# GpSimd waits for a landing after every third of its indirect transfers, in a two-layer kernel with experts

## What is computed

```python
x = x + 0.5 * L0_ffn(norm(x))      # block 0: 8 experts, F = 344, silu(g) * u, top 2
x = x +       L0_attn(norm(x))     # block 1: RWKV-like, a scan over the tokens
x = x + 0.5 * L0_ffn(norm(x))      # block 2: as block 0
x = x + 0.5 * L1_ffn(norm(x))      # block 3: 8 experts, H = 512, silu, top 2
x = x +       L1_attn(norm(x))     # block 4: retention, 16 heads of 8
x = x + 0.5 * L1_ffn(norm(x))      # block 5: as block 3
```

## Time and profile before

| what | us |
|---|---|
| median of three runs | 818.75 |
| lowest and highest | 818.47, 823.67 |
| the profiled execution | 820.56 |
| its span, first to last instruction | 818.7 |
| mean granted TensorE clock in it | 0.886 |
| DMA packets | 45119, 50.19 MB |
| of them in POOL's queue (software_dynamic) | 11776, 24.14 MB |

### The profile page before, as it was taken

How to read it: one execution, slowest core, us unless ns; L and a number is a source line. 1 busy time by engine, 2 the same in 40 slices (tenths; PEclk the granted TensorE clock), 3 DMA queues, 4 the chain that set the end, 5 groups by cost and what they waited for, 6 DMA issues and landing times.

```text
span 818.7 us, 12941 instructions
## 1 busy us (share of the span) xinstructions
PE 633.4 (77%) x4180; PEld 540.2 (66%) x4180; DVE 387.9 (47%) x1056; ACT 342.5 (42%) x667; POOL 387.3 (47%) x400
## 2 busy tenths in 40 slices
PE   2478977997489786887867875899967999966782
PEld 2377767787467785876766875766743558856772
DVE  6442115696549661514240304079688785410202
ACT  2334545654266343343445542632321324633451
POOL 1544755454544345536355354572212285456532
PEclk9998997999699898769889887999977999979887
DMA  9641122012301113112032013110030011212203
GB/s 339 198 145 34 36 71 56 27 33 62 81 27 29 23 56 91 36 49 45 28 97 65 28 36 84 38 37 8 20 87 8 21 37 33 59 39 85 61 27 113
DMA packets 45119, 50.19 MB, mean 61 GB/s; under 512 B 14456, under 2 KB 36344, under 8 KB 45056
## 3 DMA queue, kind: packets, MB, share of 16 engines
q0 software_dynamic: 11776, 24.14, 12.3%
q1 hardware_dynamic: 33280, 25.23, 9.7%
HBM read 32.04 MB, written 17.29 MB: 60 GB/s over the span
## 4 chain that ended last, share of the span: by engine, by line
PE 48%; another core or an unknown queue 10%; DVE 8%; issue 5%; ACT 4%; DMA 2%; POOL 1%; ACTq 1%; DVEq 0%; SPq 0%; POOLq 0%
PE bank L612 13%; PE bank L599 9%; PE bank L592 8%; PE pair L700 4%; PE pair L732 3%; PE bank L573 2%; PE pair L526 1%; DVE hT L1252 1%; PE pair L536 1%; ACT w_up L831 1%; DMA xs<-tokens_in,idx_in 1%; ACT hT L852 1%; PE pair L516 1%; PE bank L615 1%
## 5 line engine op out<-in xcount | busy, mean ns | idle before, releaser
L1086 POOL DMA_INDIRECT tokens_out<-ys,idx_out x184 | 189.5, 1030 | 241.4 <-ACT ys L899 194.2
L1076 POOL DMA_INDIRECT xs<-tokens_in,idx_in x184 | 188.1, 1022 | 167.3 <-PE bank L573 59.2
L612 PE MATMUL bank<-w,hT 128*128 x1288 | 191.8, 296 | 52.2 <-ACT hT L852 20.3
L612 PEld LDWEIGHTS bank<-w,hT 128*128 128x128 f32 x1288 | 175.3, 208 | 69.5 <-issue 68.6
L592 PE MATMUL bank<-xT_kept,w_up 128*128 128x128 f32 x1104 | 173.9, 307 | 47.1 <-ACT gate L849 13.2
L592 PEld LDWEIGHTS bank<-xT_kept,w_up 128*128 128x128 f32 x1104 | 157.9, 218 | 65.8 <-issue 34.7
L831 ACT ACTIVATE w_up<-w 128x728 f32 (+1 forms) x184 | 129.3, 718 | 47.1 <-DVE owner L1232 19.0
L1252 DVE TENSOR_TENSOR hT<-gate,bank 128x384 f32<-128x384 f32 x92 | 50.7, 552 | 177.0 <-PE bank L592 75.3
L599 PE MATMUL bank<-xT_kept,w_up 128*128 128x128 f32 x736 | 107.3, 296 | 17.7 <-ACT hT L852 8.1
L599 PEld LDWEIGHTS bank<-xT_kept,w_up 128*128 128x128 f32 x736 | 98.1, 207 | 26.4 <-issue 17.8
L852 ACT ACTIVATE hT<-bank 128x512 f32<-128x512 f32 x92 | 54.6, 595 | 109.9 <-PE bank L599 50.6
(11 more groups left out here) (169 smaller groups left out, 626.0 us busy)
## 6 DMA issues: line engine op xcount, KB each, us to landing
yg<-tokens_out SPq DMA_DIRECT2D x64, 128.0 KB
w<-in_w SPq DMA_DIRECT2D x8, 536.0 KB, 8.4
w<-in_w SPq DMA_DIRECT2D x8, 512.0 KB
xs<-tokens_in,idx_in POOLq DMA_INDIRECT x184
tokens_out<-ys,idx_out POOLq DMA_INDIRECT x184
tokens_in<-xn SPq DMA_DIRECT2D x8, 256.0 KB
tokens_in<-xn SPq DMA_DIRECT2D x8, 254.0 KB
out<-x SPq DMA_DIRECT2D x8, 128.0 KB
```

Source lines behind the costliest of these rows:

```text
L612: last = mm(y, hT[0:n_f, n % 2, c * P:(c + 1) * P], w_of(k, e, WD[k] + c * P, P, n_f), start=(c == 0), stop=(k == 0 and c == CH[k] - 1))
L1076: pool.indirect_dma_start(xs[:, j % RING, :], None, xn_dram[KIND[f]][b], tile_rows(idx_in, b, j))\
L1086: pool.indirect_dma_start(ys_dram[b], tile_rows(idx_out, b, j), ys[:, j % RING, :], None)\
```

## The change

Before the fourth, the seventh, the tenth transfer and so on in POOL's queue, POOL also waits until the transfer just before it has landed. `sent` is a list at build time, common to gathers and scatters of both sequences; `landed_in` and `landed_out` give the semaphore and the value that tell of a landing. The new wait stands behind the transfer's own wait. Nothing else differs.

```diff
--- before.py
+++ after.py
@@ -40,6 +40,7 @@
 NGR = len(GROUPS)
 GROUP_OF = [g for g, n in enumerate(GROUPS) for _ in range(n)]
 RING = 8
+BURST = 3
 ROUND23 = 65536.0
 WHOLE = float(1 << 23)
 UP_TO_WHOLE = (P - 1) / (2 * P)
@@ -1061,6 +1062,22 @@
 
                 return bass.IndirectOffsetOnAxis(table[:, b, j:j + 1], 0)
 
+            sent = []
+
+            def landed_in(p, j):
+
+                return ld_xs[j % RING], 16 * (ring_uses(p, j) + 1)
+
+            def landed_out(p, j):
+
+                pair, before = j // 2 % (RING // 2), j // RING * 2 + j % 2
+                return st_ys[pair], 16 * (p * stored_from(pair) + before + 1)
+
+            def breathe():
+
+                if len(sent) % BURST == 0 and sent:
+                    pool.wait_ge(*sent[-1])
+
             def gather(f, b):
                 p = PASSES.index((f, b))
                 for j in range(TILES):
@@ -1073,8 +1090,10 @@
                     if p or j >= RING:
                         before = (p, j - RING) if j >= RING else (p - 1, max(i for i in range(TILES) if i % RING == j))
                         pool.wait_ge(xT_ready, before[0] * NGR + GROUP_OF[before[1]] + 1)
+                    breathe()
                     pool.indirect_dma_start(xs[:, j % RING, :], None, xn_dram[KIND[f]][b], tile_rows(idx_in, b, j))\
                         .then_inc(ld_xs[j % RING], 16)
+                    sent.append(landed_in(p, j))
 
             def scatter(f, b):
                 p = PASSES.index((f, b))
@@ -1083,8 +1102,10 @@
                     if j == 0:
                         after(RT_DVE[b], SUB[f], "out")
                     pool.wait_ge(y_copied, p * NPAIR + j // 2 + 1)
+                    breathe()
                     pool.indirect_dma_start(ys_dram[b], tile_rows(idx_out, b, j), ys[:, j % RING, :], None)\
                         .then_inc(st_ys[j // 2 % (RING // 2)], 16)
+                    sent.append(landed_out(p, j))
```

## The result

The changed kernel takes 879.15 us, the median of four runs (875.24 to 880.87), against 818.82 us for the kernel before in the same comparison: a ratio of 1.072, 95% interval 1.067 to 1.077. It is slower by 60 us where I had forecast 42 us of gain, and it lies outside my range. All ratios are of each kernel's fast runs; left out are one run of e7 (3214.7 us), one of e8 (808.09 us) and two of the kernel before beside e8 and e9 (810.13 and 814.28 us).

What follows compares the result with a forecast made beforehand. No engine was full; 109.7 us of stalls without a releaser were blamed on long transfer runs. A 76.9 us gain less 35.3 us for blocking, late stalls and tail left 41.6: 777 us, range 748 to 808.

Steps and rivals of the forecast that it cites:

- The unknown waits: Engines standing with no releaser in the trace: 10% of the chain, 109.7 us together, to fall to 2% or less.
- The reading of them: Long unbroken runs of GpSimd's indirect transfers hold up other engines' wake-ups, by a mechanism the trace doesn't show.
- the price of one wait: GpSimd's queue: 1.43 us per exposed gather wait, 1.26 per scatter wait; 165 us for all 122 at 1.35.
- 24 us for the order in the queue: GpSimd's in-order queue: a scatter whose ys isn't ready blocks a ready gather; 3 us lost in each of 8 passes.
- 1.3 of the tail: Last scatters: one exposed wait ahead of the 367th transfer, 1.3 us, with nothing behind which to hide.
- The three stretches that GpSimd was to set: 24 to 201.5, 208 to 534 and 698 to 808 us: gains of 19.3, 49.1 and 8.5, sum 76.9 us.
- TensorE is full, no change: 534 to 598 and 629 to 698 us: 23 and 33 transfers need 40 and 57 us, so no change.
- the cover: GpSimd's existing waits, 194.2 us for ys and 59.2 for xs, 253 us to hide 165 us of new waits.
- The 10 us for stalls that begin within a group of three: Taken back from the gain for stalls still beginning inside groups of three transfers: 10 us, bounds 0 and 109.7.
- GpSimd takes it all: Rival: stalls go, but 1.72 us per transfer and queue blocking bound all passes; 812 us, chance 0.11.
- The second: Rival: stalls have another cause and stay at 109.7 us, waits add where there is no cover; 834 us, chance 0.13.
- the break is too short: Rival: with a 0.27 us pause, stalls live on from group to group and hide GpSimd's waits; 820 us, chance 0.06.

Runs made afterwards that it cites:

- e7: Against the changed kernel: each transfer waits for the landing of the third before it, queue never emptied; 695.74 us, ratio 1.022 on chip C.
- e8: Against the changed kernel: wait at every third transfer, but for the landing of the oldest of the three; 803.29 us, ratio 0.998 on chip D.
- e9: Against the changed kernel: the landing wait placed ahead of the transfer's own wait, still every third transfer; 834.58 us, ratio 1.037 on chip D.
- e6: The kernel before, unaltered, run again for its trace on chip C; 678.18 us, ratio 0.998.
- e5: The changed kernel, unaltered, timed beside the kernel before on chip C; 876.79 us, ratio 1.286.

## Why the prediction was wrong

**Right: the stalls and their end.** The unknown waits were real time, and the change removes them: 10% of the chain to 0%, and remote waits over 3 us gone. Their size with all that hangs on them is better seen now: 819 less 679, about 140 us, TensorE's lower clock included, where the pieces of the chain and five early waits gave me 109.7. The reading of them is only half right. That wake-ups of the other engines are held up is wrong. By the earlier trace rows TensorE had ended its matmuls for the gate at 215.84 us, but that end is modelled, and the semaphore update that let the gate go is recorded at 222.63, 0.02 us before the gate starts. That long runs set it off is not enough: on a chip that has the waits, the two kernels in which GpSimd stands at each landing remove them (the result and e9) and the one that hardly stands doesn't (e8), but on chip C runs of fifteen and more did nothing, three more chips have its time, and on chip A itself the runs of 12 and 13 in the stretches where TensorE is full have next to no late update. I had put that down to late wake-ups that cost nothing there.

**Wrong: the price of one wait.** This is the step that failed. I had 1.43 and 1.26 us, 1.35 in the mean, 165 us for 122. Measured, GpSimd stands 2.48 us at a landing wait where it would stand 0.30, so 2.2 us each: 0.8 us more. Two terms of the sum were too small. The release took 0.74 us, not 0.27, because the wait stands behind the transfer's own and becomes a separate instruction; e9 shows that term alone, 0.4 us. The rest is the landing, 2.61 us after the issue in the mean of 114 such waits and 3.40 in one of the pieces shown, where I had used the shortest, 2.42 and 2.25, and kept the 3.96 of the earlier trace rows as an outer bound.

Put into my own sum, as if all 122 waits were exposed (101 were), it turns the sign. A group of three takes 2 x 1.26 + (1.02 + 2.48) = 6.0 us (1.02 us is the mean busy time of a transfer after), 2.0 us per transfer, not 1.72. Then 92 x 2.0 = 184 us against 177.5, 161 x 2.0 = 322 against 326, and 59 x 2.0 = 118 against 110: 624 us of work in 613.5 us of stretch, a loss of 10 where I had a gain of 76.9. With the 24 us for the order in the queue and the 1.3 of the tail, both as predicted, that is 36 us of loss; 54.6 were measured.

The two traces divide the 54.6 us, if each stretch is taken from the start of a matmul to the start of the same matmul by its number in TensorE's order (us):

| stretch of before | before | after | measured | forecast |
|---|---|---|---|---|
| 24 to 201.5 | 175.6 | 192.7 | +17.1 | -19.3 |
| 208 to 534 | 323.2 | 321.9 | -1.3 | -49.1 |
| 534 to 598 | 64.0 | 78.5 | +14.5 | 0 |
| 629 to 698 | 68.4 | 77.2 | +8.8 | 0 |
| 698 to 808 | 107.3 | 111.8 | +4.5 | -8.5 |
| the rest | 80.2 | 91.2 | +11.0 | +1.3 |

The 34 us that I took back for blocking and late stalls stood in no stretch. The three stretches that GpSimd was to set came out at +20.3 where I had -76.9: this is the price of a wait, and in the longest the 2.0 us per transfer give 322 us, as measured. But a second term failed with it. "TensorE is full, no change" came out at +23.3 us. Of the rest, 9.2 us stand behind the start of the last matmul, where the last scatters go; I had counted one exposed wait of 1.3 us, and the chain there shows two, each with its landing. The two stretches that were full, after the change (columns as in the earlier trace rows):

```profile
551.10:629.60 78.50, 66.66 (x342) 45.22 (x341) 51.87 (x55) 18.16 (x38) 31.77 (x27) 0.93 0.08 22
661.80:738.90 77.10, 69.58 (x365) 47.33 (x364) 52.62 (x72) 23.59 (x48) 32.39 (x31) 0.95 0.11 27
```

TensorE is no longer full. It waits 11.5 us for gathers in the first of them, 10.4 of these for one that GpSimd starts at 578.25 us, behind six scatters in a row and their landing waits, and 7.4 us in the second. Its matmuls take 3 to 4 us more in each, at a granted clock of 0.93 and 0.95 against 1.00 and 0.98. My sum had asked only whether 23 and 33 transfers fit into the time, not whether each gather still comes early enough.

**Wrong: the cover.** The 253 us of GpSimd's waits that were to hide 165 us were for the most part made by the stalls: where there are none, the same two waits are 102.7 + 10.4 = 113 us (e6). I wrote that the cover shrinks if the kernel gets faster, and didn't follow it with a number. The stretches did carry part of it, by leaving the stalls out of the room.

**The smaller terms.** The 10 us for stalls that begin within a group of three were hardly needed: two remote waits are left, 1.3 and 2.9 us. TensorE's share of the chain fell from 48% to 27%. The clock did not rise, 0.886 to 0.869; TensorE waits 133.3 us for gathers where it waited 10.9.

**The rivals.** The first, "GpSimd takes it all", is what happened in kind, with its sign in the profile but for the unchanged time: the unknown waits gone, and GpSimd and landings over 15% of the chain, 51% in fact. Its time of 812 was wrong for the same reason as the forecast, 1.72 us per transfer. I had given it 0.11. The second, that the stalls have another cause than the runs, had 0.13, my own estimate. Its time of 834, with the stalls kept, didn't come, and its mark, unknown waits of 5 us and more inside groups of three, isn't there: the longest is 2.9 us. Nor do the stalls come with longer instructions of ScalarE or VectorE: between chips A and C the gate takes 489 and 487 ns, hT 552 and 551. The third, "the break is too short", fell likewise: 10% went to 0%.

**The size by chips.** Both effects are large and of opposite sign: about 140 us removed and about 196 us added on a chip with stalls, 879 against 819; nothing removed and 196 added on one without, 877 against 679. Forecasting 1.07 or 1.29 then depends on the chip, and a single trace of the kernel before doesn't tell that its stalls do.

**What stays open.** Why TensorE's semaphore updates come late, whether its matmuls do too, what differs between the chips, and whether the recording has a part in it. What in the change holds the lateness down: the emptied queue, or the slower pace of GpSimd or of all engines. Whether six or twelve in a row, or three in flight, keeps them away where they occur: 711 or 695 us there would beat both kernels. On the other four chips the kernel before is the fastest of all that ran.

## What to carry to other kernels

Here a wait for the youngest transfer cost 2.2 us of GpSimd's time and 1.6 us of the kernel, and a wait for the third-youngest 0.5 us of GpSimd's; where transfers must be held back, bound those in flight (whether that ends the stalls was not seen) and put the wait that comes true last next to the instruction that it holds (877 and 835 us, the change and e9). Before idle time is counted as cover, ask what makes it: if the change removes the cause, the cover goes with it. A stall without a releaser in a trace may belong to the chip, so the kernel before should be timed on a second one before the stall is priced.

## What the runs showed of the hardware

- The same program takes 678 to 681 us on four chips and 804 to 819 on one or two others. GpSimd's, ScalarE's and VectorE's instructions are equally long (chips A and C: a gather 1022 and 1047 ns, a scatter 1030 and 1037, the gate 489 and 487, hT 552 and 551); TensorE's are longer at the lower clock (L592: 289 ns at 0.954 and 307 ns at 0.886), and waits with no releaser in the records, 10% of the chain, stand only on the slower chips.
- Those waits are for TensorE's semaphore updates, which come up to 8.5 us after the modelled end of the matmul on chips A and D (before, e8), at most 1.8 us in the change and 1.6 in e9 there, and at most 0.02 us on chip C (e5, e6).
- They fall to 0% of the chain when GpSimd lets its transfers land before it issues more (the change and e9), and stay at 10% when it waits for the oldest of three only (e8).
- A wait that stands as an instruction of its own in GpSimd's queue is followed by 0.70 us before the transfer starts (235.07 to 235.77); one that the transfer carries, by 0.21 us (232.42 to 232.62). The order of two waits was worth some 42 us in this kernel.
